# Scores: a signal from each gather, and a wait for it ahead of the last quarter of each group's sum

## The reference

```python
scores = jnp.einsum('ehd,ehd->eh', Q[dst], mod_k) / D ** 0.5      # mod_k = K[src] + 0.2 * rel_w[edge_relations]
seg_max = jax.ops.segment_max(scores, dst, num_segments=N)
ex = jnp.exp(scores - seg_max[dst])
w = ex / denom[dst]                                               # denom: sum of ex over the edges of a node
agg = jax.ops.segment_sum(w[:, :, None] * V[src], dst, num_segments=N)
```

## Time and profile before

| | |
|---|---|
| time, median of 3 runs | 7085.9 us (7082.45 to 7089.11) |
| span of the profiled execution | 6353.0 us |
| its own time | not given apart; the median is 732.9 us above its span |
| `edge_scores`, first gather to last score | 341 to 2572 us |
| DVE, POOL, PE busy in the span | 4416.1, 4352.2, 4654.9 us |
| L653, 1664 gathers | 1712.8 us, 1029 ns each |
| L742, L745, L747, 416 each | 506.6, 507.8, 507.5 us |

### The profile page before, as it was taken

How to read it: one execution, slowest core, us unless ns; L and a number is a source line. 1 busy time by engine, 2 the same in 40 slices (tenths; PEclk the granted TensorE clock), 3 DMA queues, 4 the chain that set the end, 5 groups by cost and what they waited for, 6 DMA issues and landing times. The chain is left out here.

```text
span 6353.0 us, 69502 instructions
## 1 busy us (share of the span) xinstructions
PE 4654.9 (73%) x16402; PEld 3170.3 (50%) x16402; DVE 4416.1 (70%) x8998; ACT 2770.5 (44%) x6174; POOL 4352.2 (69%) x4103
## 2 busy tenths in 40 slices
PE   9877878787777777378888879966666666666662
PEld 5565666565666666256666644433333333343331
DVE  8867888888887777867777779945555555555557
ACT  2144444444444444288888847722222222222222
POOL 0067777777777777188787835567777777777773
PEclk9977677777777777599999989977877877767775
DMA  4489999999999999177777723355555665555554
GB/s 149 127 301 338 330 340 340 335 336 335 337 350 341 372 362 367 57 235 223 222 222 222 223 88 102 96 155 158 158 157 157 159 157 157 158 157 158 159 157 135
DMA packets 925700, 1418.46 MB, mean 223 GB/s; under 512 B 93803, under 2 KB 699235, under 8 KB 924985
## 3 DMA queue, kind: packets, MB, share of 16 engines
q1 hardware_dynamic: 705209, 749.70, 37.1%
q0 software_dynamic: 213088, 657.94, 33.4%
q10 hardware_dynamic: 7010, 6.38, 0.3%
HBM read 1140.54 MB, written 273.11 MB: 223 GB/s over the span
## 5 line engine op out<-in xcount | busy, mean ns | idle before, releaser
L653 POOL DMA_INDIRECT s_rows<-kv_rows,other x1664 | 1712.8, 1029 | 507.3 <-issue 471.1
L1401 POOL DMA_INDIRECT t_rows<-xj_rows,other x1664 | 1598.9, 961 | 523.0 <-issue 468.9
L1460 PE MATMUL ps_xsum<-t_rows,t_att 128*128 128x256 f32 x3328 | 1325.8, 550 | 783.2 <-DVE t_att L1426 783.0
L1460 PEld LDWEIGHTS ps_xsum<-t_rows,t_att 128*128 128x128 f32 x3328 | 787.3, 263 | 1321.3 <-DVE t_att L1426 1195.4
L1426 DVE SCALAR_TENSOR_TENSOR t_att<-iota,local,t_att 128x128 f32<-128x128 f32 x1664 | 579.0, 348 | 1037.9 <-ACT t_att L1416 1037.9
L1416 ACT ACTIVATE t_att<-t_att,t_rows 128x128 f32<-128x128 f32 x1664 | 531.2, 389 | 1571.4 <-DMA t_rows<-xj_rows,other 1563.9
L764 PE MATMUL ps_q<-node_tab,hot 128*128 x3328 | 1162.4, 510 | 0.0
L664 ACT ACTIVATE apart<-apart,minus_p 128x1024 bf16<-128x1024 bf16 x416 | 477.6, 1148 | 1221.5 <-DMA apart<-what_rows 1221.4
L1060 PE MATMUL ps_sum<-a_terms,a_hot 128*128 128x260 f32 x3328 | 830.3, 392 | 167.5 <-DVE node_tab L1048 155.0
L762 PE MATMUL ps_rel<-rel,hot 64*128 64x64 f32 x3328 | 583.3, 329 | 495.1 <-ACT hot L669 453.8
L1008 POOL TENSOR_TENSOR a_terms<-a_terms,score 128x1024 f32<-128x1024 f32 x416 | 786.5, 1902 | 193.4 <-DMA a_terms<-v_edges 191.5
(11 more groups left out here) (206 smaller groups left out, 3554.9 us busy)
## 6 DMA issues: line engine op xcount, KB each, us to landing
v_edges<-s_rows SPq DMA_DIRECT2D x416, 512.0 KB, 6.5
a_terms<-v_edges SPq DMA_DIRECT2D x416, 512.0 KB, 4.4
apart<-what_rows SPq DMA_DIRECT2D x416, 256.0 KB, 8.3
t_att<-a_rows SPq DMA_DIRECT2D x416, 256.0 KB, 3.5
s_rows<-kv_rows,other POOLq DMA_INDIRECT x1664, 6.0
t_rows<-xj_rows,other POOLq DMA_INDIRECT x1664, 3.2
kv_rows<-kv_out SPq DMA_DIRECT2D x97, 256.0 KB, 2.0
xj_rows<-n_hx SPq DMA_DIRECT2D x97, 130.0 KB, 2.3
```

The source lines that it names most:

```text
L653: pool.indirect_dma_start(out=rows[g % KV_RING][:, k, :], out_offset=None, in_=t["kv_rows"], in_offset=bass.IndirectOffsetOnAxis(ap=t["oth ...
L1401: pool.indirect_dma_start(out=rows[g % RING][:, k, :], out_offset=None, in_=t["xj_rows"], in_offset=bass.IndirectOffsetOnAxis(ap=t["other1 ...
L1460: nc.tensor.matmul(ps_sum[g % 4][:, k, :], att[g % ATT_RING][:, k, :], rows[g % RING][:, k, 0:D], start=True, stop=True)\
```

## The change

In groups 1 to 307 DVE's sum is cut in two: three of the four tiles first, then a wait until `described` is (g + 1) * 4 + 8, then the fourth tile. The turn of the merge follows as before. In the other groups the sum is whole. Besides, the semaphores of `softmax_numerators` join the list that `aggregate` clears.

```diff
+AHEAD = 8
@@ edge_scores
-        picked, picked_used, scored = sem("s_picked"), sem("s_picked_used"), sem("s_scored")
+        picked, picked_used, scored, described = sem("s_picked"), sem("s_picked_used"), sem("s_scored"), sem("s_described")
@@ gpsimd
                     pool.indirect_dma_start(out=rows[g % KV_RING][:, k, :], out_offset=None, in_=t["kv_rows"],
-                                            in_offset=bass.IndirectOffsetOnAxis(ap=t["other0"][:, g * U + k:g * U + k + 1], axis=0))\
+                                            in_offset=bass.IndirectOffsetOnAxis(ap=t["other0"][:, g * U + k:g * U + k + 1], axis=0),
+                                            engine_sem=described)\
                         .then_inc(rows_in[g % KV_RING], 16)
@@ vector
                 dve.wait_ge(picked_used, g + 1)
-                dve.tensor_reduce(t["score"][:, g * U * H:(g + 1) * U * H].rearrange("p (k h) -> p k h", h=H), by_head, AX.X, ALU.add)\
-                    .then_inc(scored, 1)
+                total = t["score"][:, g * U * H:(g + 1) * U * H].rearrange("p (k h) -> p k h", h=H)
+                if 1 <= g <= MERGED_AT:
+                    dve.tensor_reduce(total[:, 0:U - 1, :], by_head[:, 0:U - 1, :, :], AX.X, ALU.add)
+                    dve.wait_ge(described, (g + 1) * U + AHEAD)
+                    dve.tensor_reduce(total[:, U - 1:U, :], by_head[:, U - 1:U, :, :], AX.X, ALU.add).then_inc(scored, 1)
+                else:
+                    dve.tensor_reduce(total, by_head, AX.X, ALU.add).then_inc(scored, 1)
                 if 1 <= g <= MERGED_AT:
                     next(merging)
@@ softmax_numerators
         def sem(name):
-            return ctx.enter_context(nc.semaphore(name))
+            t["spent"].append(ctx.enter_context(nc.semaphore(name)))
+            return t["spent"][-1]
```

## The result

The changed kernel took 7091.1 us (median of 20 runs), the kernel before 7074.1 us on the same chip (20 runs). The ratio is 1.002, with a 95% interval from 1.0013 to 1.0027: slower by 14 us, between 9 and 19 (the ratio is of the means; the medians lie 17 apart). The forecast was 7008 us, faster by 78. It was wrong in sign and outside its range. Two runs further down that took far longer than the others of their kernel, one of nine of the kernel before in batch 5 (7244.4 us) and one of four with tiny passes there (13252.7 us), are left out of their ratios.

What follows compares the result with a forecast made beforehand. POOL's gathers were taken to bound edge_scores, so whatever lengthens a gather lengthens the kernel. 7085.9 - 119.7 + 40 + 1.6 = 7008 us; own range 6985 to 7035 (chance 0.68), 8 in 10 range 6975 to 7075.

Steps and rivals of the forecast that it cites:

- 732.9 us of the median lie around the span: Time outside the profiled span of 6353.0 us, taken to lie ahead of and behind everything the change touches; left unchanged.
- POOL never waits: In edge_scores, POOL's pauses between 1664 gathers stay within 0.3 us, so it never waits for rows to be scored or stored.
- the passes are not the cause: Rival, chance 0.02: something else lengthens edge_scores gathers, so moving DVE's merge passes wins nothing; 7088 us.
- The wait seldom holds: Rival, chance 0.08: late landings and PE keep DVE behind, passes stay put, a fifth of 119.7 us is won; 7064 us.
- excess, to be won: Extra gather time in the first stretch of edge_scores, beyond 957 ns each, laid to DVE's merge passes: 119.7 us.
- what is left of it: Part of the gathers' lengthening that remains because DVE's data come late in some groups: 40 us, range 17 to 67.
- clears ahead of `aggregate`: POOL clears 89 semaphores instead of 66 before its first L1008, adding 1.6 us on the path.
- passes in the window: 1.22 us DVE passes starting 0 to 0.17 us after a gather's start cost nothing; expected in two of three groups.
- DVE's waits at the quarter sum: Sign: DVE, holding the last quarter of its sum, waits 0.3 to 1 us there in most groups.
- 0.2 us of slack: In edge_scores, DVE reaches the wait 0.2 us before the gather's signal when its data are there.
- The late signal: Rival, chance 0.12: a gather's signal rises only when the next starts; passes land 0.25 us beyond the window; 7054 us.
- The signal's price: Rival, chance 0.07: each of 1664 signalling gathers costs POOL 0.08 us more, 133 us in all; 7141 us.

Runs made afterwards that it cites:

- batch 5: Kernels run on one chip of kind A, where the kernel before took 6359.1 us: the change again, tiny passes, memsets of 160 numbers in both gathering stages.
- tiny passes: Kernel before with each merge minimum and maximum in edge_scores cut to one number a partition: ratio 1.0135 on kind B, 0.9808 on kind A.
- the change again: The changed kernel, unedited, run on a chip of kind A against the kernel before there: 6259.9 us, ratio 0.9847.
- the change with the pause: Changed kernel plus a POOL memset of 256 numbers a partition after each scores-stage gather, against the kernel before on kind A: ratio 1.0591.
- longer pauses: Kernel before plus a POOL memset of 256 numbers a partition after each gather of the scores' stage, on kind B: ratio 0.9752.
- idle passes: Kernel before plus one unused 1024-element DVE minimum in each of 100 groups without a merge pass, on kind B: ratio 0.9913.
- small memset: Kernel before plus a POOL memset of 64 numbers a partition after each gather of the scores' stage, on kind B: ratio 1.0001.
- less work on PE: Kernel before with PE making one of the four relation-table products a group, from the third group on, on kind B: ratio 0.9866.
- ring of 4: Kernel before with 4 buffers of gathered rows instead of 5 (KV_RING = 4), on kind B: ratio 0.9993.

## Why the prediction was wrong

**The step that failed** is the last sentence under the sum: "732.9 us of the median lie around the span ... and I let them stand". The trace was of an execution of about 6355 us, on a chip of kind A; the time beside it, 7085.9, was of kind B. Every run here has 1.8 us outside its span. So the 732.9 us were not around the kernel but in it: on kind B some 430 us in the scores' stage and 280 in `attend`. With them fell "POOL never waits", and with that the rule that whatever lengthens a gather lengthens the kernel. No case had a price for this, so the range could not hold it. Of the rivals, "the passes are not the cause" gave nearly the time that came, 7088, by luck and by a reason that is false: the kernel before was 12 us quicker here than in the table, the change cost 14 us where this rival had 2, and the passes do lengthen the gathers, but on kind B that length is worth nothing. "The wait seldom holds" had what was seen (44 of 307 groups) and the wrong price, since it too took the excess to be worth its length.

**On kind A the working held in its main terms.** I compare the spans of two executions of that kind, the first trace and the change again: 6353.0 and 6257.6, 95.4 us.

| step | forecast | measured on kind A |
|---|---|---|
| excess, to be won | 119.7 us | 116 in the stage, 122 in the time (tiny passes) |
| what is left of it | 40 | 31 |
| clears ahead of `aggregate` | 1.6 | 1.4 |
| `aggregate` itself | 0 | -7 |
| gathers of the first stretch | 975 to 1000 ns | 981 |
| pass after a gather's start | 0.12 us | 0.07 |
| passes in the window | 2 of 3 groups | 138 of 184 |
| end of the stage | 2495 us | 2482 |
| DVE's waits at the quarter sum | 0.3 to 1 us in most groups | 0.3 to 1 us in 53 of 307, longer in 12 |
| DVE's waits for rows and PE | a third of 297.9 us | 141.5 |
| sum | -78 us | -97 (-88 to -106) |

Two things came otherwise. The quarter sum started within 0.05 us of the counted gather's end in 210 of 307 groups, so the wait held there, but mostly DVE stood for under 0.15 us: that fits the 0.2 us of slack in the forecast's working, and not the 0.3 to 1 us that it named as the sign. And 7 of the 97 us are from `aggregate`, which the forecast had not touched; the stage itself is 90 us shorter, of which the gathers' excess is 89. The traces compared here are of different chips of that kind.

DVE goes on 0.03 us after the gather's recorded end (1487.22 to 1487.25), not 0.08. The window of 0 to 0.17 us forgave that. The late signal falls: the semaphore rises with the recorded end, which the Trainium skill (Perfetto Trace Analysis, DMA Instruction — SWDGE (GPSIMD)) calls the writing of the last descriptor. The signal's price falls too: 1664 signals, ratio 0.9997, pauses still 0.30. That the passes are not the cause is refuted on kind A by the tiny passes, and the rule of the Trainium skill behind that rival (SBUF — State Buffer, Who interferes with whom) does not hold for these gathers: 1.94 us beside a `tensor_tensor` of two SBUF inputs (1005.46, the change with the pause), 0.96 when the gather begins first.

**On kind B** three things differ. PE's semaphore comes late, every fourth group where there are no passes and mostly every 4 to 26 where there are, so DVE is late, finds the count reached and seldom falls in step with the gathers. Passes then lock where they were: DVE needs 4.83 us a group (1199.59 to 1204.42), as long as three gathers of which one is lengthened (1199.63 to 1204.45), so that the pass hits the same spot again. And what is spared on the gathers returns as waits, more than once over. That the long waits hang on POOL's pace is borne out by three edits: longer pauses (0.9752) and idle passes (0.9913) slow a group down, and the tiny passes quicken it (1.0135). The pauses are the cleanest, with the small memset as their control. The pace is a condition, not the whole cause, for less work on PE moves the waits as well (0.9866).

**What stays open**: what makes a chip one of kind B (or of a batch, since no chip was seen in two), and what delays PE's semaphore. It isn't a full ring of POOL (ring of 4), nor the amount of traffic alone, for `attend` has the same waits at 140 GB/s where the scores' stage moves 290. It needs the gathers, since `aggregate` has none of it, and on the chips seen it needs them at 1.26 us apiece: at 1.45 it is gone. Between the two no pace was run on kind B. Nor is it known whether the 14 us that the change costs there have another part beside the shift from excess to waits: at the rate of the tiny passes, 7 us less excess would bring 12 us more waits, not 41. One rival is untested. The stages with late signals are also those in which the traces of kind B lack records, with the pause of 256 numbers too, and no run separates a chip that signals late from one on which the recording itself delays the signals.

No version that computes everything is the fastest on both kinds. On kind A it is the change; on kind B it is the kernel before with the pause of 256 numbers (0.9752), and in its scores' stage it would cost 289 us on kind A (2520 against 2231).

## What to carry to other kernels

Before a profile is used for a sum, hold its span against the time it is to explain; where they differ by more than what an execution needs outside its span (1.8 us here), the profile is of another execution, and its slack is not this one's. A stall that is proved in the trace is worth its length only where nothing else is late: cut the cause out as a whole (the tiny passes) and time that first, as it is the most that any repair can bring. And a filler on the queue of a producer is a cheap probe of whether its pace is itself the trouble; it has to be timed on every kind of chip that the kernel will meet, since here the same filler gained 2.5% on one and costs 289 us of the stage on the other.

## What the runs showed of the hardware that was not expected

- Chips, each seen in one batch, differ in kind and not only by a few tenths of a per cent: the same kernel takes 6357.6 and 6359.1 us on two chips and 7075 to 7126 on three others, with all of the difference in the stages that gather (434 us in the scores, 282 in `attend`).
- On the slower kind PE's signal can come 12 us after its last product while PE works on, and the next group's comes with it (2556.66 and 2561.54, both used only from 2568.62 on).
- On the slower kind, more work can be faster: 1664 memsets of 0.33 us took 2.5% off the time (6946.5 us against 7126.2).
- A memset on POOL of 64 numbers a partition between two gathers costs nothing (0.17 us, inside the pause of 0.30).
- `engine_sem` on an indirect gather rises 0.03 us after its recorded end or sooner, and 1664 of them cost nothing that can be measured.
- Placing an instruction of 1.22 us against the gathers works to about 0.01 us: 129 of 184 passes started 0.06 to 0.08 us after a gather's start, and with the pause changed all 184 started 0.12 ahead of one. The same wait is worth -97 us at a pause of 0.30 us and +95 us at 0.49.
- On kind B the records of semaphores and of landings are partly missing (no time to landing for the gathers), which marks such a trace at a glance.
